# A fused state-space, attention and feed-forward layer on one core: merged head transfers, the weights' peaks two chunks sooner, and four smaller moves of work

## The chip, the cores and the metric

The kernel runs on one core of a Trainium2 chip. The metric is the device time of one execution in microseconds; lower is better.

## The reference

The input `x` holds complex weights for 32 images (32 x 128 x 64), `txt` holds 77 rows of 1024 for each image.

```python
h = tok(log_dt, Lambda, x, 1024)          # (32, 128, 1024): real part of sum_n W[n] * exp(dt*Lambda[n]*pos)
h = concatenate([h, txt], axis=1)         # (32, 205, 1024)
h = h + attn(layernorm(h), wq, wk, wv, wo)   # 32 query heads on 8 key/value heads of 32, causal softmax
h = h + ffn(layernorm(h), W_base, b_base, enc0, enc1, coefs, masks)
# ffn: x @ (W_base + low-rank update through a real Fourier matrix).T + b
```

## The kernel before

The program has three stages, each a block of its own with one instruction stream per engine; the streams meet only through semaphores, and each stage begins when all engines have left the one before.

**Stage 1 (`ssm`)** makes the 128 image rows of each of the 32 images. It goes over 16 chunks of 8 rows (`NCH`, `ch`): GpSimd and VectorE form `u` and `es`, TensorE multiplies, ScalarE copies the result into `ob`, and SP stores it to `hcat` with four transfers a chunk (L180). SP also loads `wq`, `wk` and `wv` ahead for stage 2 (L169). In chunks 4 to 15 VectorE takes one twelfth of the weights' absolute maxima each (`weight_peak`, L370), and after chunk 15 reduces them to `peaks` (L388, L389). SP writes `peaks` to memory (L174), waits, and reads them back broadcast to all partitions (L176) in its turn for chunk 15, ahead of that chunk's stores.

**Stage 2 (`attention`)** is a pipeline over the images in steps `b` = -4 to 32. In step b, where the image exists: attention proper of image b (`att`: `scores` L956 and L959, exponentials L758, causal masks L684 on GpSimd, high parts L765 on ScalarE, low parts `pl` L689 on GpSimd for k = 1, 2 and L911 on VectorE for k = 0, products `weigh` L986, `norm` L808 and L811); the row maxima of image b+1 (`max`: `score_rows` L1000 to L1007, `take_maxes` L854 and L860); the projections of image b+2 (`qkv`: `unit` L1018 to L1026); the turned and split x of image b+3 (`turn`); the layer norm of image b+4 (`ln`); the load of image b+5. A number is kept as two float16 parts, a high one and the rest. Each step has eight slots `g`, one per group of four heads. The steps -4 to -1 fill the pipeline, from step 30 on there are no projections, and in step 31 no maxima either.

Projected heads come out of TensorE with 128 features (four heads of 32) on the partitions, in `qsh`, `qsl`, `ksh` and `ksl`; the score products want one head's 32 features three times below each other (high, high, low). SP's `restack` moves them with transfers inside SBUF, one per head r of four and per part k: twelve transfers for each half of q and of k, so 48 a step (L572). The negated maxima (`mh`, `ml`, unit "m") go in as two more rows (`shift_rows`, L617 and L618). All these, the turning transfers (`turn`, L623 and L624) and, in step -1, the loads for stage 3 (`ahead`, L597: wo, 4 MB, and 14 small ones) stand in one order in SP's stream: q and k of the second half, m 1, in step -1 the loads, turn, k and q of the first half, m 0. ScalarE's first part of the norm's split (`high_part`, L717 and L719, slots 4 to 7) overwrites the x that the latest turn reads, and waits for it.

The reciprocal root of the norm starts on VectorE (`rsqrt_guess`, L1108 to L1110) and ends with three rounds of four small instructions and `nmean` on GpSimd (`scale_rows`, L1117 to L1120, L661). In step -4 VectorE then makes the low parts `ql` of wq (`weights_low`, L794), and after them the low parts `xfl` of x (`low_part`, L837); TensorE's first projection in step -2 waits for their turned form. In step 31 VectorE also has `spare_work` for stage 3.

**Stage 3 (`tail`)** goes over 52 tiles of 128 rows: two projections (L1381 to L1383), residual, norm, store.

## Time and profile before

| | |
|---|---|
| median of 3 runs | 2941.69 us (2940.85 to 2944.85) |
| profiled execution | 2947.19 us, its span 2945.1 us |
| TensorE matmul busy | 2695.8 us, 92% |
| VectorE, ScalarE, GpSimd busy | 66%, 41%, 39% |
| stage 1, stage 2, stage 3 | about 0 to 187, 187 to 1797, 1797 to 2945 us |
| granted TensorE clock, mean | 0.969 |

The span runs from the first to the last instruction. A granted clock of 1.00 is TensorE's full speed of 2.4 GHz, 0.50 is 1.2 GHz. Matmuls overlap and their ends are modelled, so a busy share near 100% is not the array at its peak. In a row of the timeline the columns are the start, the time, the engine, the line with its operation, what is written and read, the count, and in brackets how long the engine sat idle before it and what ended that. SPq and ACTq rows are the issue of a transfer, not its course.

### The profile page before, as it was taken

What the parts mean: (1) busy time and instruction counts of PE and PEld (TensorE: products, weight loads), DVE (VectorE), ACT (ScalarE), POOL (GpSimd) and SP (SyncE); (2) the same over time, 40 slices, a digit from 0 to 9 for tenths busy, and PEclk for the clock granted to TensorE, in tenths of its full rate; (3) what the DMA queues carried; (4) which work ended last, traced back from release to release, by engine and by line L of the source; (5) the groups of instructions that cost most, each with busy time, mean ns of one, the idle gap of its engine ahead of it and who ended that gap; (6) DMA issues with size and microseconds to landing.
All of it is one profiled execution on the core that took longest, in us unless ns stands there. A gap on an engine that the chain in (4) does not pass through costs nothing. (4 is left out here: it accounts for less than half of the span.)

```text
span 2945.1 us, 70977 instructions
## 1 busy us (share of the span) xinstructions
PE 2695.8 (92%) x27456; PEld 1949.7 (66%) x27456; DVE 1940.4 (66%) x5569; ACT 1201.6 (41%) x2506; POOL 1144.2 (39%) x1811
## 2 busy tenths in 40 slices
PE   1948699999999999999999986999999999999999
PEld 1837589989898998989899972444444444444444
DVE  8964488887888888788888774744444444444443
ACT  4342466676766767666666663101010100101010
POOL 2751266565656656566565563101111010101110
PEclk9978899999999999999999995899999999999999
DMA  7754534434343443435344325354554555454543
GB/s 240 190 123 112 87 88 96 98 77 98 82 102 85 93 98 77 99 82 103 81 95 87 66 55 178 79 139 115 136 123 128 131 119 134 119 140 115 136 122 81
DMA packets 564334, 324.72 MB, mean 110 GB/s; under 512 B 501016, under 2 KB 519704, under 8 KB 563520
## 3 DMA queue, kind: packets, MB, share of 16 engines
q1 hardware_dynamic: 541488, 256.35, 39.2%
q10 hardware_dynamic: 22512, 63.84, 6.9%
q8 instruction: 219, 3.59, 0.5%
q14 instruction: 115, 0.94, 0.1%
HBM read 116.49 MB, written 80.61 MB: 67 GB/s over the span
## 5 line engine op out<-in xcount | busy, mean ns | idle before, releaser
L1018 PE MATMUL psJ<-xth,qh 128*128 128x205 f16 x2048 | 520.3, 254 | 52.4 <-DMA xtl<-xfl 46.9
L689 POOL TENSOR_TENSOR pl<-arena,ph 128x410 f16<-128x410 f32 (+1 forms) x512 | 499.5, 995 | 94.7 <-ACT ph L765 94.7
L1020 PE MATMUL psJ<-xth,ql 128*128 128x205 f16 x2048 | 519.0, 253 | 0.0
L1019 PE MATMUL psJ<-xtl,qh 128*128 128x205 f16 x2048 | 518.6, 253 | 0.0
L684 POOL TENSOR_SCALAR_AFFINE_SELECT arena<-arena 128x256 f32<-128x256 f32 (+1 forms) x768 | 331.6, 438 | 475.5 <-ACT arena L758 454.5
L1243 POOL TENSOR_TENSOR arena<-stage,arena 128x1024 f32<-128x1024 f32 x52 | 122.2, 2349 | 938.1 <-DVE stage L1286 938.1
L1257 ACT CAST xh<-arena 128x1024 f16<-128x1024 f32 x52 | 54.3, 1045 | 998.3 <-DVE arena L1295 998.3
L758 ACT ACTIVATE arena<-psT,escale 128x410 f32<-128x410 f32 (+1 forms) x768 | 401.1, 567 | 119.0 <-PE psT L959 59.7
L765 ACT CAST ph<-arena 128x410 f16<-128x410 f32 (+1 forms) x768 | 334.8, 500 | 15.8 <-POOL arena L684 15.5
L1286 DVE SCALAR_TENSOR_TENSOR stage<-ps5O,osc,h_in 128x512 f32<-128x512 f32 x104 | 78.0, 751 | 390.6 <-PE ps5O L1383 390.6
L860 DVE TENSOR_REDUCE mx<-psS 77x2 f32<-77x410 f32 x512 | 295.4, 577 | 39.8 <-PE psS L1007 32.3
L1381 PE MATMUL ps5F<-wfh,xth 128*128 128x512 f16 x832 | 315.4, 379 | 3.1 <-DMA xtl<-xl 2.0
L1382 PE MATMUL ps5O<-wol,ath 128*128 128x512 f16 x832 | 316.3, 380 | 0.0
L1381 PE MATMUL ps5O<-woh,ath 128*128 128x512 f16 x832 | 316.3, 380 | 0.0
L1383 PE MATMUL ps5O<-woh,atl 128*128 128x512 f16 x832 | 316.2, 380 | 0.0
L854 DVE CUSTOM_DVE_ANT_0 seen<-psS,mask 128x128 bf16<-128x128 f32 x1024 | 235.3, 286 | 121.5 <-PE psS L1000 121.5
L1382 PE MATMUL ps5F<-wfl,xth 128*128 128x512 f16 x832 | 315.3, 379 | 0.0
L1383 PE MATMUL ps5F<-wfh,xtl 128*128 128x512 f16 x832 | 315.3, 379 | 0.0
L986 PE MATMUL psO<-vh,ph 128*128 128x33 f16 (+1 forms) x3072 | 261.2, 178 | 5.1 <-issue 4.7
L986 PE MATMUL psO<-vl,ph 128*128 128x33 f16 (+1 forms) x3072 | 260.4, 178 | 0.0
L986 PE MATMUL psO<-vh,pl 128*128 128x33 f16 (+1 forms) x3072 | 260.4, 178 | 0.0
L986 PEld LDWEIGHTS psO<-vh,ph 128*128 128x128 f16 (+1 forms) x3072 | 245.2, 97 | 7.3 <-issue 6.3
(234 smaller groups left out, 6143.7 us busy)
## 6 DMA issues: line engine op xcount, KB each, us to landing
a_in<-acat SPq DMA_DIRECT2D x52, 512.0 KB, 3.8
h_in<-hcat SPq DMA_DIRECT2D x52, 512.0 KB, 4.6
qst<-qsh SPq DMA_DIRECT2D x512, 51.2 KB, 2.1
out<-stage SPq DMA_DIRECT2D x51, 512.0 KB, 3.1
hcat<-ob SPq DMA_DIRECT2D x64, 256.0 KB, 4.5
xin<-hcat ACTq DMA_DIRECT2D x32, 512.0 KB
acat<-arena ACTq DMA_DIRECT2D x64, 256.0 KB
qst<-qsl SPq DMA_DIRECT2D x256, 51.2 KB, 2.5
```

The costliest lines, as they stand in the source:

```text
L684: pool.affine_select(out=v, in_=v, compare_op=ALU.is_ge, fill=0.0, base=0, pattern=[[0, v.shape[1]], [1, w]], channel_multiplier=-1).then_ ...
L689: pool.tensor_tensor(view(pl, g % 2, k), view(p32, g % 2, k), view(ph, g % 2, k), ALU.subtract).then_inc(lo_pool, 1)
L758: act.activation(view(p32, g % 2, k), ps_view(psT[(g + k) % 2], k), ACT.Exp, scale=(escale[:, 0:1] if k < 2 else escale[0:TXT, 0:1])).then ...
L765: act.copy(view(ph, g % 2, k), view(p32, g % 2, k)).then_inc(hi_done, 1)
L860: dve.tensor_reduce(dst, v, AX.X, ALU.max).then_inc(s_read, 1)
L986: m = pe.matmul(o[:, t, r, :], p, v[0:T[j], j, g, :], start=n == 0, stop=n == len(list_) - 1)
L1018: pe.matmul(ps[:, 0:S], wh[:, k, c], xth[:, par, k, 0:S], start=k == 0, stop=False)
L1019: pe.matmul(ps[:, 0:S], wh[:, k, c], xtl[:, par, k, 0:S], start=False, stop=False)
L1020: m = pe.matmul(ps[:, 0:S], wl[:, k, c], xth[:, par, k, 0:S], start=False, stop=k == KC - 1)
L1381: pe.matmul(ps[h][:], th[:, k, :], wh[:, k, c], start=k == 0, stop=False)
L1382: pe.matmul(ps[h][:], th[:, k, :], wl[:, k, c], start=False, stop=False)
L1383: m = pe.matmul(ps[h][:], tl[:, k, :], wh[:, k, c], start=False, stop=k == KC - 1)
```

## The change

- **Merged head transfers.** The columns of `wq` and `wk` are laid out, ahead of the launch, so that a chunk's partitions hold feature and head as d*4 + r. `restack` then moves a whole part with one transfer: 3 for a half of q or k, 12 a step, each of the bytes of four before. `qst` is laid out as [half, r, c] and `mx` likewise, so the operands of `scores` for two heads become two runs of 205 columns.
- **Peaks.** The twelve reductions stand in chunks 2 to 13, the two final ones at the end of chunk 13; SP writes the peaks ahead of chunk 14's stores and reads them back ahead of chunk 15's.
- **First root.** In step -4 the three rounds and `nmean` are VectorE's, right behind the guess; GpSimd does none in that step.
- **Loads for stage 3.** They stand in step 1 instead of step -1, between m 1 and the turn as before.
- **Last steps.** In steps 30 and 31 (`LATE` on) the low part for k = 1 is VectorE's (`lo_late`), GpSimd keeps k = 2.

```diff
             for ch in range(NCH):
-                if ch == NCH - 1:
+                if ch == NCH - 2:
                     sp.wait_ge(peaks_ok, 1)
                     sp.dma_start(acat[0, 0:2 * P].rearrange("(p t) -> p t", t=2), peaks[:]).then_inc(peaks_out, 16)
+                if ch == NCH - 1:
                     sp.wait_ge(peaks_out, 16)
...
                 dve.tensor_tensor(u[:, ch % 2], u[:, ch % 2], u2[:, ch % 2], ALU.add).then_inc(u_ok, 1)
-                if ch >= NCH - 12:
-                    weight_peak(ch - (NCH - 12))
-            dve.wait_ge(piece_ok, 12)
-            dve.tensor_reduce(peaks[:, 0:1], pieces[:, 0:8], AX.X, ALU.max)
-            dve.tensor_reduce(peaks[:, 1:2], pieces[:, 8:12], AX.X, ALU.max).then_inc(peaks_ok, 1)
+                if NCH - 14 <= ch < NCH - 2:
+                    weight_peak(ch - (NCH - 14))
+                if ch == NCH - 3:
+                    dve.wait_ge(piece_ok, 12)
+                    dve.tensor_reduce(peaks[:, 0:1], pieces[:, 0:8], AX.X, ALU.max)
+                    dve.tensor_reduce(peaks[:, 1:2], pieces[:, 8:12], AX.X, ALU.max).then_inc(peaks_ok, 1)
...
         mh, ml = sb("mh", [NH // 2, 2, S], F16), sb("ml", [NH // 2, 2, S], F16)
-        qst = [sb(f"qst{i}", [STACK + 2, NH, S], F16) for i in range(2)]
+        qst = [sb(f"qst{i}", [STACK + 2, 2, REP, NKV // 2, S], F16) for i in range(2)]
         kst = [sb(f"kst{i}", [STACK + 2, NKV, S], F16) for i in range(2)]
...
         pl = sb("pl", [P, 2, 3, 2 * S], F16)
-        mx = sb("mx", [P, 2, NH])
+        mx = sb("mx", [P, 2, 2, REP, NKV // 2])
         seen = sb("seen", [P, REP, P], BF16)
...
         cleared, lo_pool, mask_ok, late_ok = sem("cleared"), sem("lo_pool"), sem("mask_ok"), sem("late_ok")
+        lo_late = sem("lo_late")
         pool_c, dve_c, dve_ln, const_ok = sem("pool_c3"), sem("dve_c3"), sem("dve_ln"), sem("const_ok")
...
+        LATE = B - 2
+        def by_pool(n):
+            return 2 * n - max(0, n - 8 * LATE)
...
             if kind == "q":
-                wait(eng, q_in[n // 4], 16 * 12 * (b + 2))
+                wait(eng, q_in[n // 4], 16 * 3 * (b + 2))
             if kind == "k":
-                wait(eng, k_in[n], 16 * 12 * (b + 2))
+                wait(eng, k_in[n], 16 * 3 * (b + 2))
             if kind == "v":
...
                 for k, src in enumerate(parts_):
-                    rows = dst[k * HD:(k + 1) * HD].rearrange("d (c r) i -> d c r i", r=4)
-                    for r in range(4):
-                        sp.dma_start(rows[:, cs, r, :], src[r * HD:(r + 1) * HD, cs, :]).then_inc(arrived, 16)
+                    sp.dma_start(dst[k * HD:(k + 1) * HD], src[:, cs, :]).then_inc(arrived, 16)
...
                     wait(sp, pj_lo, before(b - 1, nxt) + at(units(prev), "k", 1) + 1)
-                    restack(K_PARTS, kst[nxt], slice(1, 2), k_in[1])
+                    restack(K_PARTS, kst[nxt][:, 4:8], slice(1, 2), k_in[1])
                     wait(sp, pj_lo, before(b - 1, nxt) + at(units(prev), "q", NKV - 1) + 1)
-                    restack(Q_PARTS, qst[nxt], HALVES[1], q_in[1])
+                    restack(Q_PARTS, qst[nxt][:, 1], HALVES[1], q_in[1])
                 if has["att"]:
...
                     shift_rows(1, par)
-                if b == -1:
-                    sp.wait_ge(w_lo, 2 * KC)
+                if b == 1:
...
                     wait(sp, st_filled, 24 * b + 12)
-                    restack(K_PARTS, kst[par], slice(0, 1), k_in[0])
+                    restack(K_PARTS, kst[par][:, 0:4], slice(0, 1), k_in[0])
                     wait(sp, pj_lo, base + at(rows, "q", 3) + 1)
-                    restack(Q_PARTS, qst[par], HALVES[0], q_in[0])
+                    restack(Q_PARTS, qst[par][:, 0], HALVES[0], q_in[0])
                 if has["max"]:
...
             def shift_rows(half, to):
-                heads = slice(half * (NH // 2), (half + 1) * (NH // 2))
-                sp.dma_start(qst[to][STACK:STACK + 1, heads, :], mh[:, half, :]).then_inc(m_in[half], 16)
-                sp.dma_start(qst[to][STACK + 1:STACK + 2, heads, :], ml[:, half, :]).then_inc(m_in[half], 16)
+                sp.dma_start(qst[to][STACK:STACK + 1, half], mh[:, half, :]).then_inc(m_in[half], 16)
+                sp.dma_start(qst[to][STACK + 1:STACK + 2, half], ml[:, half, :]).then_inc(m_in[half], 16)
...
                 if not has["att"]:
-                    if has["ln"]:
+                    if has["ln"] and b > -4:
                         scale_rows(b)
...
                                            channel_multiplier=-1).then_inc(masked, 1)
-                    for k in (1, 2):
+                    for k in (1, 2) if b < LATE else (2,):
                         pool.wait_ge(hi_done, 24 * b + 3 * g + k + 1)
...
-                            if k:
-                                wait(act, lo_pool, 16 * b + 2 * (g - 2) + k)
+                            last = 8 * b + g - 2
+                            if k == 1 and last >= 8 * LATE:
+                                act.wait_ge(lo_late, last + 1 - 8 * LATE)
+                            elif k:
+                                wait(act, lo_pool, by_pool(last + 1) - 2 + k)
                             else:
...
                     rsqrt_guess(chain, dve, rs, mv[:, :, 1])
+                    if b == -4:
+                        rsqrt_rounds(link, dve, rs)
+                        dve.tensor_scalar(nmean[:], mv[:, :, 0], -1.0, None, ALU.mult).then_inc(ln_done, 1)
...
                             m = dve.tensor_tensor_reduce(seen[:, r, :], src[:, r * P:(r + 1) * P], mask[:, 0, :], 1.0, LEAST,
-                                                         ALU.add, ALU.max, mx[:, 0, 4 * j + r:4 * j + r + 1])
+                                                         ALU.add, ALU.max, mx[:, 0, j // 4, r, j % 4:j % 4 + 1])
                         m.then_inc(s_read, 1)
...
                         v = src[0:TXT, 0:2 * S].rearrange("p (h i) -> p h i", i=S)
-                        dst = mx[0:TXT, 1, 4 * j + 2 * k - 2:4 * j + 2 * k]
+                        dst = mx[0:TXT, 1, j // 4, 2 * k - 2:2 * k, j % 4]
                         dve.tensor_reduce(dst, v, AX.X, ALU.max).then_inc(s_read, 1)
...
                                           ALU.subtract).then_inc(lo_done, 1)
+                        if b >= LATE:
+                            dve.wait_ge(hi_done, 24 * b + 3 * g + 2)
+                            dve.tensor_tensor(view(pl, g % 2, 1), view(p32, g % 2, 1), view(ph, g % 2, 1),
+                                              ALU.subtract).then_inc(lo_late, 1)
                     for j in groups[1:]:
...
                 if k < 2:
-                    m = pe.matmul(ps[:, 0:2 * S], K[:, g, 0:P], Q[:, 4 * g + 2 * k:4 * g + 2 * k + 2, :],
+                    m = pe.matmul(ps[:, 0:2 * S], K[:, g, 0:P], Q[:, g // 4, 2 * k:2 * k + 2, g % 4, :],
                                   start=True, stop=True)
                 else:
-                    m = pe.matmul(ps[0:TXT, 0:REP * TXT], K[:, g, P:S], Q[:, 4 * g:4 * g + 4, P:S],
+                    m = pe.matmul(ps[0:TXT, 0:REP * TXT], K[:, g, P:S], Q[:, g // 4, :, g % 4, P:S],
                                   start=True, stop=True)
...
                 pe.wait_ge(lo_done, 8 * b + g + 1)
-                pe.wait_ge(lo_pool, 16 * b + 2 * g + 2)
+                pe.wait_ge(lo_pool, by_pool(8 * b + g + 1))
+                if b >= LATE:
+                    pe.wait_ge(lo_late, 8 * (b - LATE) + g + 1)
...
-                pe.wait_ge(q_in[j // 4], 16 * 12 * (b + 1))
-                pe.wait_ge(k_in[j // 4], 16 * 12 * (b + 1))
+                pe.wait_ge(q_in[j // 4], 16 * 3 * (b + 1))
+                pe.wait_ge(k_in[j // 4], 16 * 3 * (b + 1))
                 K, Q = kst[par], qst[par]
...
                     for r in range(REP):
-                        m = pe.matmul(ps[:, r * P:(r + 1) * P], Q[0:STACK, 4 * j + r, 0:P], K[0:STACK, j, 0:P],
+                        m = pe.matmul(ps[:, r * P:(r + 1) * P], Q[0:STACK, j // 4, r, j % 4, 0:P], K[0:STACK, j, 0:P],
                                       start=True, stop=True)
...
                     for r in range(2):
-                        m = pe.matmul(v[:, r, :], Q[0:STACK, 4 * j + 2 * (k - 1) + r, P:S], K[0:STACK, j, :],
+                        m = pe.matmul(v[:, r, :], Q[0:STACK, j // 4, 2 * (k - 1) + r, j % 4, P:S], K[0:STACK, j, :],
                                       start=False, stop=r == 1, skip_group_check=True)
...
-                    heads = slice(n * (NH // 2), (n + 1) * (NH // 2))
                     pe.wait_ge(s_read, 24 * (b + 1) + 12 * (1 - n))
-                    pe.transpose(ps[0:NH // 2, 0:P], mx[:, 0, heads], ident[:])
-                    m = pe.transpose(ps[0:NH // 2, P:S], mx[0:TXT, 1, heads], ident[0:TXT, 0:TXT])
+                    pe.transpose(ps[0:NH // 2, 0:P], mx[:, 0, n].rearrange("p r c -> p (r c)"), ident[:])
+                    m = pe.transpose(ps[0:NH // 2, P:S], mx[0:TXT, 1, n].rearrange("p r c -> p (r c)"), ident[0:TXT, 0:TXT])
                 if last:
...
             a = a.T
+        if name in ("L0_attn_wq", "L0_attn_wk"):
+            a = a.reshape(D, -1, 4, HD).transpose(0, 1, 3, 2).reshape(D, -1)
         a = np.ascontiguousarray(a)
```

## Rows read from the trace of the kernel before

**Rows 1.** Busy time in a stretch of the steady steps.

```profile
core 0: us, PE busy (x) PEld busy (x) DVE busy (x) ACT busy (x) POOL busy (x), PEclk, DMA share, GB/s
700.00:1000.00 300.00, 287.44 (x4374) 267.98 (x4372) 246.33 (x841) 197.97 (x447) 182.52 (x334) 1.00 0.41 88
```

**Rows 2.** TensorE's waits, whole span: total, times, longest.

```profile
PE psJ L1018 <- DMA xtl<-xfl: 46.9, 1, 46.9
PE psS L1004 <- DVE mx L854: 43.4, 64, 1.1
...
PE psT L956 <- DMA qst<-ml: 16.8, 2, 12.1
PE psS L1004 <- DVE mx L860: 14.0, 1, 14.0
```

**Rows 3.** Timeline, steps -1 and 0: TensorE, VectorE and SP's queue.

```profile
266.13 0.61 PE L1000 MATMUL psS<-kst,qst 96*128 96x128 f16 x4 [5.89 <-DMA qst<-qsl]
...
280.74 0.59 SPq L597 DMA_DIRECT2D stage<-in_L_attn_wo  x1
...
282.88 11.87 SPq L597 DMA_DIRECT2D mk<-in_L_ffn_mask  x1
...
294.89 0.35 DVE L866 SCALAR_TENSOR_TENSOR ml<-psJ,mh 16x205 f16<-16x205 f32 x1
...
305.80 1.28 SPq L623 DMA_TRANSPOSE xth<-xfh  x1
...
327.74 0.59 SPq L618 DMA_DIRECT2D qst<-ml  x1
```

**Rows 4.** Timeline of ScalarE: the first high part in steps -1, 0, 1.

```profile
310.62 0.72 ACT L717 ACTIVATE xin<-xin,nmean 128x512 f32<-128x512 f32 x1 [17.17 <-DMA xtl<-xfl]
...
362.19 0.70 ACT L717 ACTIVATE xin<-xin,nmean 128x512 f32<-128x512 f32 x1
...
408.68 0.71 ACT L717 ACTIVATE xin<-xin,nmean 128x512 f32<-128x512 f32 x1
```

**Rows 5.** Timeline, step 1: ml of slot 0, and its issue.

```profile
386.26 0.35 DVE L866 SCALAR_TENSOR_TENSOR ml<-psJ,mh 16x205 f16<-16x205 f32 x1
...
390.55 0.60 SPq L617 DMA_DIRECT2D qst<-mh  x1
```

**Rows 6.** Timeline, step -4: VectorE and GpSimd.

```profile
198.29 0.19 DVE L1110 TENSOR_SCALAR rs<-rs 128x2 int32<-128x2 int32 x1
198.52 9.65 DVE L794 SCALAR_TENSOR_TENSOR ql<-stage,qsc,qh 128x1024 f16<-128x1024 f32 x8
198.59 1.26 POOL L1117 TENSOR_TENSOR rs<-rs 128x2 f32<-128x2 f32 x1
...
209.41 0.25 POOL L661 TENSOR_SCALAR nmean<-mv 128x2 f32<-128x2 f32 x1
...
215.36 0.75 DVE L837 SCALAR_TENSOR_TENSOR xfl<-xin,rs,xfh 77x512 f16<-77x512 f32 x1 [0.62 <-ACT xfh L719]
```

**Rows 7.** Timeline, end of stage 1: ScalarE and SP's queue.

```profile
178.04 0.59 ACT L246 COPY ob<-ps 128x512 f32<-128x512 f32 x1 [1.14 <-PE ps L401]
179.63 0.34 SPq L176 DMA_DIRECT2D arena<-acat  x1
180.02 3.19 SPq L180 DMA_DIRECT2D hcat<-ob  x4
```

**Rows 8.** Busy time after a wait, in a slot of step 30, in step 31.

```profile
266.00:275.00 9.00, 8.87 (x66) 7.96 (x67) 3.17 (x13) 0.69 (x2) 0.00 (x0) 0.66 0.11 25
...
1739.20:1742.40 3.20, 2.51 (x57) 1.95 (x54) 3.06 (x14) 2.76 (x7) 2.87 (x6) 1.00 0.33 79
1765.50:1789.50 24.00, 15.74 (x272) 9.18 (x271) 20.69 (x35) 19.69 (x43) 21.84 (x35) 0.50 0.11 37
```

**Rows 9.** All instructions of L911: nanoseconds min/median/max, first and last start.

```profile
L911 DVE TENSOR_TENSOR pl<-arena,ph x256: 562/586/1690, 334.7 to 1789.4; 128x410 f16<-128x410 f32 x128
```

**Rows 10.** Transfers: count, KB each, us from issue to landing.

```profile
qst<-qsh SPq DMA_DIRECT2D x512, 51.2 KB, 2.1
...
hcat<-ob SPq DMA_DIRECT2D x64, 256.0 KB, 4.5
```

## The prediction

> **What bounds the kernel.** I read the windows first. In the middle of attention TensorE is busy 287.4 of 300 us at the full clock [rows 1]; each step there takes 46.5 us, the distance between the same ScalarE instruction of two steps [rows 4]. Nothing can be gained there except what TensorE waits for, so the second view is the list of its waits [rows 2]. Of these only one belongs to the steady steps, the 43.4 us for L854 (64 times, two a step, about 0.7 us each), and the change doesn't shorten what L854 does. Its waits on a transfer are few and long: they stand at the start (46.9 us for the first turned x, 12.1 for ml, and 5.9 for qsl [rows 3]), and one of 4.7 us (16.8 less 12.1) for ml again, which is at the end. The third view, the timeline with SP's queue, says why: a restack is 12 issues of some 0.65 us, and SP does nothing else meanwhile; in step -1 the loads that are needed only 1.4 ms later are put between two restacks and hold the queue from 280.7 to 305.8 us [rows 3]. ScalarE then waits 17.2 us for the turned x behind them [rows 4], and TensorE 14.0 us through L860 [rows 2]. The steady steps hide the SP queue, the fill doesn't.
>
> **The change, part by part** (minus is a gain).
>
> 1. *Peaks sooner.* SP writes the peaks after chunk 14's rows, waits, reads them at 179.63 and starts chunk 15's four stores at 180.02, while ScalarE's last copy was done at 178.04 + 0.59 = 178.63 [rows 7]. The round trip now lies one chunk ahead, so the stores start at 178.7: -1.3. The reductions move two chunks ahead, where VectorE has as much room; the first needs wq, whose load I take as landed; if it were not, the cost is that lateness less VectorE's idle time. I put 0 on it.
>
> 2. *First root on VectorE.* GpSimd's thirteen small steps run from 198.59 to 209.66; the first took 1.26 us beside VectorE [rows 6]. VectorE's own step on two columns takes 0.19 us, 0.23 from start to start, so thirteen take about 2.9 us and ScalarE can begin 8 us sooner. But VectorE does them ahead of its eight ql parts (9.65 us), which stand before its first xfl. Before, the last xfl ended at 216.1 [rows 6]; now the root ends at 198.5 + 2.9 = 201.4, ql at 211.1, and four xfl (0.75 us each, about 0.66 from start to start) at 213.7. The same 2.4 us pass on to kl, to the second image's norm and to TensorE's second start. Gain -2.4, not 8; bounds 0 and -8.
>
> 3. *Merged restacks.* One restack becomes 3 issues; at 0.65 us an issue that is 2 us instead of 8. At the start, TensorE waits 5.9 us for qsl [rows 3]; this restack and the one ahead of it shrink by 6 us each, so the wait is gone: -5.9. The wait for ml (12.1) starts after step -1's work. Step -1 began at 266.1; ml was ready at 295.2, 29.1 us later, yet went out at 327.7 behind turn and restacks [rows 3]. It lands about 2 us after, so the wait began near 317.6, and TensorE's own work in this step is 317.6 - 266.1 - 14.0 = 37.5 us. With the queue free, mh and ml are issued (1.2) and landed (2) at 29.1 + 3.2 = 32.3 us, ahead of 37.5: -12.1. In the steady steps the gain is 0, because no wait on a transfer stands there to be shortened. What lies behind 0: SP ended its steady restack at 390.55 without anybody waiting [rows 5].
>
> 4. *Small loads leave step -1.* The 25 us of SP go, so ScalarE's wait goes and TensorE's with it: -14.0 [rows 2, 4].
>
> 5. *Clock.* After the 5.9 us wait TensorE ran nine microseconds at a mean clock of 0.66 [rows 8]: 9 x 0.34 = 3.1 us lost. The lower level is 0.50, 1.2 GHz. This restart goes (-3.0); the two others end in short or stalled work, and I take -1.5 each: -6.0.
>
> 6. *Small loads come into step 1.* This is the cost. SP takes them up when mh and ml of slot 0 are ready, 386.6 us on the old time axis, and not at 390.55, since its restack is shorter [rows 5]. Two issues 1.2, then the loads. Before, from the first of these loads to ScalarE's release were 310.62 - 280.74 = 29.9 us [rows 3, 4]. Release: 386.6 + 1.2 + 29.9 = 417.7. ScalarE wants that turned x at 408.68 [rows 4]: 9.0 us late. In step -1 17.2 us of ScalarE's wait became 14.0 of TensorE's; here the next exponentials stand behind the waiting instruction, and I take 8.0, between 6 (the same slack of 3.2) and 9. The wait lets the clock fall: a restart as in part 5, 2.5. Sum +10.5. The restack and mh, ml behind the loads would be 9 us late too, but TensorE's next step is then 8 us late itself. The bound below is 0 (the loads drain quicker), above 17 + 3 (the stall of step -1 again).
>
> 7. *Two last steps.* TensorE's 4.7 us wait for ml [rows 2], which SP issues behind a restack, goes, with 1.5 of clock: -6.2. Against it, in step 30 VectorE is busy 3.06 of 3.20 us of a slot, GpSimd 2.87 [rows 8]. Taking a low part (1.0 us) off GpSimd while VectorE gains one of 0.586 us [rows 9], 0.54 taken, since starts follow a little closer than durations, makes VectorE the bound: 8 x 0.54 = +4.3. In step 31 VectorE was busy 20.7 of 24.0 us; with seven or eight more it needs 24.7, while GpSimd falls well below its 21.8 [rows 8]. I take 0, between -3 (GpSimd alone had set the pace) and +2. Part: -1.9; bounds -9 and +0.
>
> The two-piece operand of L956 (two runs of 205 instead of one of 410), the strided writes into mx, and the permuted weights, which are laid out ahead of the launch, I cost at 0: no row shows such a run, the nearest are the steady waits, which leave TensorE no stall there. Above it 2 us.
>
> One rule speaks against part 3. The Trainium skill, "DMA: Bandwidth & Descriptors", section Issuing engines are not separate DMA queues, says that the time a sequencer needs to initiate a DMA is usually small relative to the DMA. Here the queue's rows say otherwise: issues of 0.65 us one after another, landing 2.1 us after each [rows 10]. By the rule parts 3 and 5 would shrink; it is a rival below.
>
> **Sum.** -1.3 - 2.4 - 5.9 - 12.1 - 14.0 - 6.0 + 10.5 - 1.9 = -33.1. The profiled execution took 2947.2 (span 2945.1), which gives 2914.1; the runs' median is 2941.7, 0.2% lower, so 2941.7 - 33.1 = 2908.6.
>
> **Rivals.**
>
> A. *The loads are free in step 1.* The queue in a steady step carries less once restacks are merged. Then part 6 is 0: 2898. Against it: the 4 MB alone blocked SP for 11.9 us in one issue [rows 3].
>
> B. *The next wait takes over in the fill.* VectorE and ScalarE have long serial stretches there, and part 3's 12.1 or part 4's 14.0 could be half eaten: +9, or the loads cost the full 17 + 3 in step 1 (+10): 2917.
>
> C. *Bytes, not issues.* A merged transfer lands as late as its four pieces did; parts 3 and 5 give nothing (22 us back): 2930. This is the rule cited above. For it: DMA engines are busy 41% in the steady window [rows 1]. Against: 256 KB of hcat land in 4.5 us, 51 KB in 2.1 [rows 10].
>
> D. *VectorE and GpSimd hold each other up in the last steps.* One L911 took 1.69 us instead of 0.586 [rows 9]. If all 16 new ones did, +17: 2925. The Trainium skill, "SBUF — State Buffer", section SBUF: two separate sides, calls the port pair that both share an exclusive lock; the 1.69 us agrees with that, the median of 0.586 says that it is rare.
>
> E. *The other side: slower.* A merged transfer moves at the rate of one small one, 4 x 2.1 = 8.4 us, and six a step, one after another, need 50.4 us against a step of 46.5 [rows 4, 10]: +3.9 in 30 steps, less the gain of the fill: about 3025. It decides from 7.9 us a transfer, (46.5 + 1.1) / 6. Against it the 4.5 us for 256 KB.
>
> F. *It doesn't do what it says:* something else in the fill (the first weights, the first norm) ends each wait, all within 5 us of before: 2938.
>
> **How the numbers follow.** Forecast 0.50 (own range 2901 to 2915), A 0.16, B 0.14, C 0.05, D 0.08, E 0.04, F 0.03. The range of 8 in 10 holds the forecast, A and B with the bounds of parts 6 and 7: 2894 to 2921. A measurement here tells 0.2%, 5.9 us, from no change. Faster: all but E and F, 0.93; within: F, 0.03; slower: E, 0.04.
>
> **What would show it.** SP's restacks as 3 issues, about 2 us; the loads in step 1 with a new wait of ScalarE of about 9 us at its high part and of TensorE of about 8, at half clock after it; no wait of TensorE on ml or qsl; L860's 14.0 gone; ScalarE's first xfh some 10 us sooner but TensorE's first projection only 3 to 4; a slot of step 30 at 3.7 us with VectorE without idle time. The prediction is wrong if the steady steps change from 46.5 us (E, or a gain that I exclude), if the new wait in step 1 is under 4 or over 14, or if step -1 keeps a wait of more than 5 us.

## The result and the profile after

The changed kernel takes 2913.9 us in the median of 4 runs (2910.36 to 2916.59); the kernel before took 2943.27 beside it (2940.85 to 2945.48). The ratio is 0.99 with an interval of 0.9883 to 0.9917, a gain of 29.4 us. The profiled spans are 2945.1 and 2911.4 us, 33.7 apart; the forecast was 33.1 off the profiled time.

TensorE's waits over the whole span, the view of [rows 2], now for the changed kernel:

```profile
PE psJ L1040 <- DMA xtl<-xfl: 46.6, 1, 46.6
PE psS L1026 <- DVE mx L870: 45.7, 65, 1.1
PE psT L979 <- ACT arena L770: 25.6, 42, 11.8
PE psO L1008 <- DVE pl L931: 7.4, 6, 2.0
```

L1026, L870 and L979 are the L1004, L854 and L959 of before. The waits for ml and qsl and the 14.0 us behind L860 are gone. One is new: 11.8 us for ScalarE's exponentials (L770). SP's queue and ScalarE in step 1 of the changed kernel show where it comes from, in the columns of [rows 3]:

```profile
344.68 0.58 SPq L626 DMA_DIRECT2D qst<-mh  x1
...
345.94 1.20 SPq L607 DMA_DIRECT2D stage<-in_L_attn_wo  x1
...
348.91 11.77 SPq L607 DMA_DIRECT2D mk<-in_L_ffn_mask  x1
360.73 5.77 SPq L607 DMA_DIRECT2D cf<-in_L_ffn_coefs  x1
...
373.47 1.28 SPq L632 DMA_TRANSPOSE xth<-xfh  x1
...
378.92 0.64 SPq L583 DMA_DIRECT2D kst<-ksh  x1
379.60 0.60 SPq L583 DMA_DIRECT2D kst<-ksl  x1
380.25 0.60 SPq L583 DMA_DIRECT2D kst<-ksh  x1
```
```profile
378.30 0.72 ACT L726 ACTIVATE xin<-xin,nmean 128x512 f32<-128x512 f32 x1 [11.47 <-DMA xtl<-xfl]
```

The reader sees three things. A restack of k is three issues of 0.6 us. The loads hold the queue for 27.5 us (345.94 to 373.47), much as they did in step -1 (25.1, [rows 3]). And ScalarE, which waits for nothing else, stands 11.5 us for the turned x behind them.

To place gains I use one mark that every kernel has, ScalarE's mh, which is written once for each half of an image's maxima: the second half early in the image's own step, the first half late in the step before. Here are its rows in the changed kernel, for the second half of images 0, 1 and 2 (steps 0, 1 and 2), the first half of image 29 (late in step 28) and the second half of image 31 (step 31):

```profile
296.00 0.33 ACT L783 ACTIVATE mh<-psJ 16x205 f16<-16x205 f32 x1
...
342.47 0.33 ACT L783 ACTIVATE mh<-psJ 16x205 f16<-16x205 f32 x1
...
402.27 0.33 ACT L783 ACTIVATE mh<-psJ 16x205 f16<-16x205 f32 x1
...
1638.87 0.33 ACT L783 ACTIVATE mh<-psJ 16x205 f16<-16x205 f32 x1 [0.45 <-PE psJ L1056]
...
1728.49 0.33 ACT L783 ACTIVATE mh<-psJ 16x205 f16<-16x205 f32 x1
```

The table takes the distances between such rows, for all kernels that ran ("projection" is the start of TensorE's first projection of x; "step 2 to 29" ends at the mark late in step 28, some 26.5 steps on; "rest" is the span less the mark of step 31, which stands where that step begins, so step 31 itself lies in the rest). The distance from step 0 to step 1 is 46.5 us in all.

| kernel | projection | step 0 | step 1 to 2 | step 2 to 29 | step 29 to 31 | rest |
|---|---|---|---|---|---|---|
| before | 224.91 | 337.93 | 46.68 | 1241.76 | 92.58 | 1179.7 |
| changed | 223.51 | 296.00 | 59.80 | 1236.60 | 89.62 | 1182.9 |
| loads_back | 228.50 | 311.74 | 46.96 | 1237.07 | 90.86 | 1178.1 |
| loads_end0 | 225.64 | 296.44 | 47.70 | 1237.04 | 90.52 | 1178.3 |
| low_on_gpsimd | 227.16 | 298.70 | 59.64 | 1238.05 | 86.28 | 1176.8 |
| end0_low | 226.18 | 298.01 | 47.20 | 1236.31 | 86.29 | 1180.1 |
| four_pieces | 224.15 | 310.84 | 67.71 | 1238.11 | 93.66 | 1178.4 |
| merge_only | 221.65 | 309.62 | 46.59 | 1239.44 | 86.29 | 1176.0 |
| before_loads1 | 225.11 | 313.57 | 67.63 | 1241.46 | 94.10 | 1176.3 |
| memset_wait | 221.53 | 294.40 | 59.71 | 1235.89 | 90.85 | 1178.2 |
| best | 220.01 | 291.93 | 46.59 | 1236.22 | 86.34 | 1179.5 |
| best_root_gpsimd | 223.54 | 297.70 | 46.48 | 1236.73 | 86.32 | 1179.8 |

From before to changed: -41.9 at step 0, +13.1 from step 1 to 2, -5.2 over the steady steps, -3.0 at the end, +3.2 in the rest: with a step of rounding, the 33.7 us of the spans.

### The profile page after: what moved, and what is told of

The parts are those of the page before. It is cut to its first block and busy times, and to the rows that moved or that the text cites. A ratio compares the mean times of both kernels' runs of the same rounds, so it can differ in the third digit from the quotient of the medians.

```text
span 2911.4 us, 69838 instructions
## 1 busy us (share of the span) xinstructions
PE 2689.6 (92%) x27456; PEld 1945.8 (67%) x27456; DVE 1955.2 (67%) x5598; ACT 1202.3 (41%) x2506; POOL 1125.5 (39%) x1782
## 3 DMA queue, kind: packets, MB, share of 16 engines
q1 hardware_dynamic: 449328, 256.28, 42.1%
## 5 line engine op out<-in xcount | busy, mean ns | idle before, releaser
L1040 PE MATMUL psJ<-xth,qh 128*128 128x205 f16 x2048 | 518.1, 253 | 49.6 <-DMA xtl<-xfl 46.6
L698 POOL TENSOR_TENSOR pl<-arena,ph 128x410 f16<-128x410 f32 (+1 forms) x496 | 489.8, 1006 | 100.5 <-ACT ph L777 100.5
L770 ACT ACTIVATE arena<-psT,escale 128x410 f32<-128x410 f32 (+1 forms) x768 | 402.0, 566 | 113.1 <-PE psT L979 60.0
L777 ACT CAST ph<-arena 128x410 f16<-128x410 f32 (+1 forms) x768 | 334.8, 500 | 12.4 <-POOL arena L693 12.1
L876 DVE TENSOR_REDUCE mx<-psS 77x2 f32<-77x410 f32 x512 | 296.5, 579 | 44.2 <-PE psS L1029 37.5
L870 DVE CUSTOM_DVE_ANT_0 seen<-psS,mask 128x128 bf16<-128x128 f32 x1024 | 235.4, 286 | 98.2 <-PE psS L1022 98.2
L1008 PEld LDWEIGHTS psO<-vh,ph 128*128 128x128 f16 (+1 forms) x3072 | 245.6, 97 | 10.5 <-DVE pl L927 8.4
## 6 DMA issues: line engine op xcount, KB each, us to landing
qst<-qsh SPq DMA_DIRECT2D x128, 205.0 KB, 4.7
qst<-qsl SPq DMA_DIRECT2D x64, 205.0 KB, 5.6
```

What stands on the lines that cost most here:

```text
L698: pool.tensor_tensor(view(pl, g % 2, k), view(p32, g % 2, k), view(ph, g % 2, k), ALU.subtract).then_inc(lo_pool, 1)
L770: act.activation(view(p32, g % 2, k), ps_view(psT[(g + k) % 2], k), ACT.Exp, scale=(escale[:, 0:1] if k < 2 else escale[0:TXT, 0:1])).then ...
L777: act.copy(view(ph, g % 2, k), view(p32, g % 2, k)).then_inc(hi_done, 1)
L876: dve.tensor_reduce(dst, v, AX.X, ALU.max).then_inc(s_read, 1)
L1008: m = pe.matmul(o[:, t, r, :], p, v[0:T[j], j, g, :], start=n == 0, stop=n == len(list_) - 1)
L1040: pe.matmul(ps[:, 0:S], wh[:, k, c], xth[:, par, k, 0:S], start=k == 0, stop=False)
```

## The experiments

The kernel before was run again beside them: it took 2943.36 us (9 runs) beside the first four, 2941.01 (21) beside four_pieces, merge_only, before_loads1 and memset_wait, and 2943.39 (9) beside best and best_root_gpsimd. Ratios are against these. Diffs are against the changed kernel unless said otherwise.

### loads_back: the small loads in step -1 again

```diff
-                if b == 1:
+                if b == -1:
+                    sp.wait_ge(w_lo, 2 * KC)
                     for dst, src, arrived in ahead:
```

> The changed kernel with the loads for stage 3 back in step -1; merged restacks stay. Theory (SP's queue sets the waits): the loads now start near 257 us instead of 281, ScalarE's turned x is released 29.9 us later, near 287, about 7 us after it is due, and mh, ml of the first image land near 297; step 0 begins at 296 to 298 instead of 287.5, and the 11.8 us wait in step 1 is gone. Against before -33 us (2910), 3 to 4 us faster than the changed kernel. Rival (my part 4: the loads in step -1 cost their 14.0 whatever the restacks are): step 0 begins at 301 or later, against before -28 or less.

Measured: 2913.48 us (2909.81 to 2914.54), ratio 0.9889 (0.9876 to 0.9903). The step 0 mark comes 15.7 us later than in the changed kernel, and 12.8 of the 13.1 us in step 1 are saved. 5.0 of the 15.7 us stand ahead of the first projection, which this edit doesn't touch. A move that I counted at -14 + 10.5 is worth nothing here. Neither theory nor rival came out whole: step 0 began at 303.7, as the rival had it (298.7 without those 5.0 us), the gain over the kernel before is 29.9 us, and the kernel is 0.4 us faster than the changed one and not 3 to 4. TensorE's waits in this kernel:

```profile
PE psT L979 <- ACT arena L770: 12.0, 42, 0.9
PE psS L1026 <- DVE mx L876: 7.6, 1, 7.6
```

Even with the loads back in step -1, the 14.0 us behind L860 have become 7.6 (L876 is that line), for SP, with less to issue ahead of them, reached the loads at 260.4 instead of 280.7:

```profile
260.44 0.61 SPq L607 DMA_DIRECT2D stage<-in_L_attn_wo  x1
...
262.69 10.67 SPq L607 DMA_DIRECT2D mk<-in_L_ffn_mask  x1
...
288.55 1.27 SPq L632 DMA_TRANSPOSE xth<-xfh  x1
```

### loads_end0: the same loads at the end of SP's turn in step 0

```diff
-                if b == 1:
-                    for dst, src, arrived in ahead:
-                        sp.dma_start(dst, src).then_inc(arrived, 16)
...
                 if has["max"]:
                     wait(sp, pj_lo, base + at(rows, "m", 0) + 1)
                     shift_rows(0, nxt)
+                if b == 0:
+                    for dst, src, arrived in ahead:
+                        sp.dma_start(dst, src).then_inc(arrived, 16)
```

> The changed kernel with the loads for stage 3 at the end of step 0's turn in SP's queue, behind mh and ml of slot 4, instead of step 1's between mh, ml and the turn. Theory (the loads block what stands right behind them, and behind that place there are some 20 us of room): no wait of TensorE over 3 us in steps 0 to 2, step 0 still begins at 287.5; 13 us faster than the changed kernel, -42 against before (2901). Rival (the bytes of the loads hold up the transfers behind them wherever they stand): ScalarE still waits over 5 us for a turned x, gain over the changed kernel under 6.

Measured: 2901.42 us (2898.64 to 2903.98), ratio 0.9851 (0.9837 to 0.9865), 12.5 us under the changed kernel. SP's queue in this kernel:

```profile
324.10 0.59 SPq L622 DMA_DIRECT2D stage<-in_L_attn_wo  x1
...
326.20 10.31 SPq L622 DMA_DIRECT2D mk<-in_L_ffn_mask  x1
...
347.81 0.68 SPq L622 DMA_DIRECT2D mk<-in_L_ffn_mask  x1
348.59 0.62 SPq L583 DMA_DIRECT2D kst<-ksh  x1
...
353.84 1.28 SPq L631 DMA_TRANSPOSE xth<-xfh  x1
```

The loads begin 22 us earlier than in the changed kernel, in time that the queue would have idled or spent on restacks with slack (there it did nothing from 323.6 to 331.4), so the turn goes out at 353.8 and not at 373.5. The distance from step 1 to 2 is 47.7 us against 46.7 before: the loads now cost 1 us (47.2, 46.6 and 46.5 in the three other kernels that have them here).

### low_on_gpsimd and end0_low: the low parts stay on GpSimd

```diff
-        LATE = B - 2
+        LATE = B
```

end0_low has this edit and that of loads_end0.

> The changed kernel with all low parts for k = 1 and 2 on GpSimd again, in steps 30 and 31 too. Theory (VectorE is the bound in both steps): a slot of step 30 takes 3.2 us instead of 3.6 to 4.1, TensorE's clock stays up in it, step 31 takes 28.4 instead of 29.7; 4 to 6 us faster than the changed kernel, -34 against before. Rival (GpSimd was the bound in these steps, moving work off it paid): 1 to 4 us slower than the changed kernel.

> Both of the two edits before: loads at the end of step 0, low parts on GpSimd. They lie 1.3 ms apart, so the theory has them add up: 17 to 19 us faster than the changed kernel, -47 against before (2896). If either rival holds, its part is missing: -34 or -42.

Measured: 2907.3 us (2905.27 to 2911.28), ratio 0.9872 (0.9858 to 0.9887), and 2894.86 (2893.68 to 2899.69), ratio 0.9831 (0.9817 to 0.9845). Each is 6.6 us under its counterpart with VectorE's low parts. In the table the last steps take 86.3 us in the five kernels with merged restacks and the low parts on GpSimd, and 89.6 to 90.9 in the four with them on VectorE. Windows over step 30 of the changed kernel and over the same step of low_on_gpsimd, in the columns of [rows 1]:

```profile
1698.60:1728.50 29.90, 23.81 (x421) 17.87 (x417) 27.20 (x107) 23.36 (x53) 22.27 (x32) 0.80 0.23 47
```
```profile
1702.00:1728.50 26.50, 20.69 (x428) 16.09 (x427) 23.49 (x99) 23.11 (x52) 23.79 (x41) 1.00 0.27 59
```

With the low parts on VectorE it is busy 27.2 of 29.9 us; with them on GpSimd no engine is busy over 23.8 of 26.5. TensorE's granted clock averages 0.80 in the first and 1.00 in the second. The low parts themselves were not held up, as all instructions of their line show (nanoseconds min/median/max):

```profile
L931 DVE TENSOR_TENSOR pl<-arena,ph x16: 567/576/855, 1699.4 to 1754.7; 128x410 f16<-128x410 f32 x16
```

### four_pieces: the merged layout, but twelve issues again

```diff
-                    sp.dma_start(dst[k * HD:(k + 1) * HD], src[:, cs, :]).then_inc(arrived, 16)
+                    for i in range(4):
+                        if cs.stop - cs.start == 4:
+                            c = cs.start + i
+                            sp.dma_start(dst[k * HD:(k + 1) * HD, :, i, :], src[:, c, :]).then_inc(arrived, 16)
+                        else:
+                            sp.dma_start(dst[k * HD + 8 * i:k * HD + 8 * i + 8], src[32 * i:32 * i + 32, cs, :]).then_inc(arrived, 16)
```

> The changed kernel with each merged restack issued in four pieces again: the same bytes, layout and packets as the merged ones, but twelve issues a half-step where the changed kernel has three. Theory (what the merging bought is SyncE's issue time, about 0.65 us for each of the issues taken away): the restacks take about 8 us a half-step again, TensorE waits some 4 us for the q rows at the start of step -1 and some 8 us for ml, and the 5 us that the steady steps gained are gone (from the first mh of step 2's second half to that of step 29's first half 1286 us, not 1281); so 8 to 10 us under the kernel before, 2934. Rival (the gain comes from the landing of the merged layout, not from the issues): the time stays at the changed kernel's, 2914.

Measured: 2945.33 us (2937.38 to 2947.69), ratio 1.0013 (1.0004 to 1.0022): all of the gain is gone, and more than I expected. The bytes and the layout are those of the changed kernel, so the rival falls. The packets are not, against what the expectation says: SP's queue moved 535344 here and 449328 in the changed kernel. That the time goes by issues and not by packets or bytes is seen in the issues themselves, which take 0.6 us each whether they carry 51.2 or 205.0 KB. TensorE's waits in this kernel:

```profile
PE psT L984 <- ACT arena L775: 26.0, 41, 13.7
...
PE psT L981 <- DMA qst<-ml: 12.9, 3, 5.0
...
PE psS L1027 <- DMA qst<-qsl: 6.3, 1, 6.3
```

Against the changed kernel the table has +14.8 us at step 0, +7.9 from step 1 to 2 (here SP reaches the loads later, and they cost 21.0 us instead of 13.1), +1.5 over the steady steps and +4.0 at the end. The 1286 and 1281 us of the expectation end one image later, at the mark late in step 29: that distance is 1286.0 us before, 1280.8 in the changed kernel and 1282.3 here, so of the steady gain of 5 us, which I had expected to go, 1.5 went. On the whole I had expected 11 us less. 7.9 us that I hadn't counted are the loads' cost in step 1, which I took as independent of the issues; the rest is not placed, for its profiled execution was the quickest of its runs, 8 us under the median, and its span understates it.

### merge_only: nothing but the merging

```diff
-                if ch == NCH - 2:
+                if ch == NCH - 1:
...
-                if NCH - 14 <= ch < NCH - 2:
-                    weight_peak(ch - (NCH - 14))
-                if ch == NCH - 3:
+                if NCH - 12 <= ch:
+                    weight_peak(ch - (NCH - 12))
+                if ch == NCH - 1:
...
-                if b == 1:
+                if b == -1:
+                    sp.wait_ge(w_lo, 2 * KC)
...
-                    if has["ln"] and b > -4:
+                    if has["ln"]:
...
-                    if b == -4:
-                        rsqrt_rounds(link, dve, rs)
-                        dve.tensor_scalar(nmean[:], mv[:, :, 0], -1.0, None, ALU.mult).then_inc(ln_done, 1)
```

(and LATE = B as above)

> The changed kernel with all else put back: small loads in step -1, low parts on GpSimd up to the end, the first root on GpSimd, the weights' peaks in chunks 4 to 15. Only the merged restacks are left. Theory (once the restacks are merged, the loads' place, the root and the low parts give nothing or cost): -33 us against the kernel before, about 2910, no slower than the whole change. Rival (the parts add up as I predicted: without the loads' move, the root and the low parts the merging alone is worth less): above 2920.

Measured: 2905.05 us (2903.98 to 2906.5), ratio 0.9877 (0.9863 to 0.989). Merging alone gains 36.0 us, against 29.4 for the whole change. The step 0 mark is 28.3 us earlier than before, the last steps are 6.3 us shorter, the steady steps 2.3; behind the first projection no wait of over 6 us is left in the fill.

### before_loads1: the loads' move alone

Against the kernel before:

```diff
-                if b == -1:
-                    sp.wait_ge(w_lo, 2 * KC)
+                if b == 1:
```

> The kernel before with one edit: the small loads issued in step 1 in place of step -1, the restacks unmerged. Theory (the loads' step costs the step that takes them, wherever it is, and with the long restacks it costs more in step 1 because SyncE's turn is longer there): 25 us less at the end of step 0, 13 to 27 us more in step 1: 2943, within 4 us of the kernel before. Rival (my prediction's parts 4 to 6, which were summed as if independent of the merging): -14 -1.5 +10.5, 5 us or more under it, 2938 or less.

Measured: 2941.67 us (2935.04 to 2945.89), ratio 0.9999 (0.999 to 1.0008). 24.4 us are won at step 0 and 21.0 lost from step 1 to 2. TensorE's waits:

```profile
PE psT L958 <- ACT arena L757: 30.8, 47, 14.4
...
PE psT L955 <- DMA qst<-ml: 13.8, 3, 4.9
PE psS L999 <- DMA qst<-qsl: 6.3, 1, 6.3
```

The 12.1 us for ml are gone here with the restacks unmerged (the longest wait is 4.9): the loads and the restacks had made that wait together, and either edit takes most of it.

### memset_wait: GpSimd's memset behind the root

In the changed kernel one of VectorE's small steps in the first root took some 25 times as long as the others. VectorE, then GpSimd:

```profile
195.33 0.16 DVE L1139 TENSOR_TENSOR rs<-rs 128x2 f32<-128x2 f32 x1
195.53 4.18 DVE L1140 TENSOR_SCALAR rs<-rs 128x2 f32<-128x2 f32 x1
199.74 0.16 DVE L1141 TENSOR_TENSOR rs<-rs 128x2 f32<-128x2 f32 x1
...
210.37 2.73 DVE L853 SCALAR_TENSOR_TENSOR xfl<-xin,rs,xfh 128x512 f16<-128x512 f32 x4
```
```profile
195.43 2.17 POOL L679 MEMSET ph<- 128x2460 f16 x1
197.54 2.14 POOL L680 MEMSET pl<- 128x2460 f16 x1
```

The edit, ahead of the memset of ph:

```diff
+                        pool.wait_ge(ln_done, 1)
```

> The changed kernel with one wait more: GpSimd's memset of ph and pl in step -4 waits for the end of the first root's rounds on VectorE. Theory (the VectorE instruction of 4.18 us among rounds of 0.16 us is held up by GpSimd's memsets): that instruction takes 0.2 us, the first TensorE projection begins 4 us sooner (about 219.5 us), and so does step 0; 4 us under the changed kernel, 2910. Rival (the next wait takes over: the q weights or the turned x are late anyway, or the memset itself comes late): under 1 us.

Measured: 2908.45 us (2907.46 to 2911.4), ratio 0.989 (0.9876 to 0.9903). The same instruction takes 0.17 us, as its fellows do:

```profile
196.11 0.16 DVE L1140 TENSOR_TENSOR rs<-rs 128x2 f32<-128x2 f32 x1
196.30 0.17 DVE L1141 TENSOR_SCALAR rs<-rs 128x2 f32<-128x2 f32 x1
```

The projection starts 2.0 us sooner than in the changed kernel, and 4.7 sooner than the mean of the five kernels with the collision in one piece (226.2, the changed kernel among them). (The sixth, four_pieces, started it at 224.15.) By the times alone it can't be told from the changed kernel, since the two intervals overlap; the trace shows the mechanism.

### best and best_root_gpsimd: the parts that paid, together

best is end0_low with memset_wait's edit. best_root_gpsimd is end0_low with the first root back on GpSimd:

```diff
-                    if has["ln"] and b > -4:
+                    if has["ln"]:
...
-                    if b == -4:
-                        rsqrt_rounds(link, dve, rs)
-                        dve.tensor_scalar(nmean[:], mv[:, :, 0], -1.0, None, ALU.mult).then_inc(ln_done, 1)
```

> The merged restacks, the small loads at the end of SyncE's turn in step 0, the low parts on GpSimd to the end, the first root on VectorE and GpSimd's first memset behind its rounds. Theory (the memset's collision with the root is worth its 4 us here too): 4 us under the same kernel without the wait, 2891. Rival (the turned x comes late for another reason, and the first projection begins no more than 2 us sooner): 2893 to 2895.

> The kernel best with the first root computed on GpSimd, as in the kernel before, and no extra wait. Theory (from the last of the root's start values on VectorE to the last low part of x, 17.6 us passed with the root on GpSimd, 18.8 with it on VectorE beside GpSimd's memsets, 15.0 with the memset held back): 2.6 us later than best at the first projection, so 2 to 3 us over best in the span. Rival (nothing of it reaches the end, the run to run spread of stage 1 is larger): within 1 us of best.

Measured: 2888.45 us (2888.07 to 2890.11), ratio 0.9817 (0.9803 to 0.983), 54.9 us under the kernel before; and 2893.78 (2889.3 to 2895.62), ratio 0.9829 (0.9816 to 0.9843). The runs of the two overlap a little at 2889 to 2890, and their profiled spans are 2887.1 and 2893.5. best is 6.4 us under end0_low, where I had expected 4. The two lie 5.3 us apart, where I had expected 2 to 3: from the end of the guess to the last xfl it is 14.8 against 17.6 us, 2.8 as expected, and the rest is not explained. best_root_gpsimd and end0_low are 1.1 us apart with overlapping intervals: with the collision, no gain from the root on VectorE is shown. TensorE's waits in best:

```profile
PE psJ L1040 <- DMA xtl<-xfl: 43.2, 1, 43.2
...
PE psT L979 <- ACT arena L770: 17.2, 46, 1.8
```

## Why the prediction was right, and where it was not

The forecast of 2908.6 us lies 5.3 under the median, in its own range, and the range of 8 in 10 holds the result. The mechanism ahead of step 0 was right in the main: the waits named are gone, and where parts 1 to 5 summed to -41.7, the mark in step 0 moved -41.9. That the two agree to 0.2 us is luck. Ahead of the first projection, where parts 1 and 2 had -3.7, it moved -1.4; from there to step 0, where parts 3 to 5 had -38.0, -40.5. The -1.4 is itself a lucky draw: in the six kernels with the root on VectorE and the memsets beside it the projection starts at 223.51 (the changed kernel) to 228.50, 225.9 in the mean, and before it started at 224.91. The agreement of the whole hides several terms that were off.

1. *Peaks sooner* (-1.3). This came as worked. SP starts chunk 15's stores at 177.54, 0.03 us after ScalarE's last copy ends at 177.51, where it was 1.39 us after before (178.63 to 180.02, [rows 7]): -1.4 for -1.3. With the peaks early that distance is 0.02 to 0.03 us in all nine kernels, with them late 1.2 to 1.4 in the three. That the copy itself ended 1.1 us sooner doesn't go with the edit: its end lies between 177.3 and 179.4 in the twelve kernels, earliest in merge_only, which has the peaks late.

```profile
176.93 0.58 ACT L247 COPY ob<-ps 128x512 f32<-128x512 f32 x1 [1.14 <-PE ps L403]
177.54 3.02 SPq L181 DMA_DIRECT2D hcat<-ob  x4
```

2. *First root on VectorE* (-2.4). The order of work was right: root, then ql, then xfl. From the end of the guess to the end of the last xfl, it took 17.6 us before (198.48 to 216.11, [rows 6]), and 18.8 in the changed kernel (194.31 to 213.10), because one instruction stood 4.2 us beside GpSimd's memsets. With the memset held back (memset_wait) it took 14.8, from 195.09 to 209.87: -2.8 for the -2.4 as worked. The term that failed is the duration of the thirteen steps, 2.9 us expected and 6.5 measured: in the changed kernel part 2 gave a loss of 1.2 us there and not a gain. I had thought of two engines holding each other up for the last steps only, as rival D; it struck here.

3. and 4. *Merged restacks* (-5.9 -12.1) and *small loads leave step -1* (-14.0). The sum was right, the shares were not. From projection to the step 0 mark it is 113.0 us before, 88.0 with merging alone, 88.5 with the move alone, 72.5 with both: each alone is worth 25, together 40.5. So 9 us, most of them the wait for ml, could be had by either, and I had given them to the merging. That matters for the next step.

5. *Clock* (-6.0). No restart is left in step -1: the granted clock was 0.66 over nine microseconds [rows 8], now it is 1.00 in a window of the same length. How much of the step 0 gain is clock can be read from TensorE's busy time between the first projection and the mark of step 0, for the same 723 matmuls: 76.35 us before and 68.31 now, 8.0 less where I had 6.0. The other 32.5 of the 40.5 us are idle time. (The ends of matmuls are modelled, so the split is rough.) The kernel before, then the changed one, whose last two rows are for part 5 and part 6:

```profile
224.91:337.93 113.02, 76.35 (x723) 71.64 (x724) 43.18 (x149) 28.76 (x59) 11.76 (x45) 0.81 0.44 101
```
```profile
223.51:296.00 72.49, 68.31 (x723) 65.49 (x724) 42.59 (x147) 28.79 (x59) 10.99 (x41) 0.97 0.55 92
...
256.00:265.00 9.00, 8.78 (x92) 8.45 (x92) 6.37 (x21) 1.31 (x4) 0.00 (x0) 1.00 1.05 153
...
378.50:390.00 11.50, 9.68 (x137) 8.79 (x138) 6.10 (x18) 9.75 (x20) 5.94 (x10) 0.71 0.68 123
```

6. *Small loads come into step 1* (+10.5). It cost 13.1. ScalarE was 11.5 us late and not 9.0, nearly all of it came through to TensorE (11.8, not 8.0), and the clock after it, 0.71 over 11.5 us in the last row above, took 3.3 and not 2.5. The two make 15.1, 2.0 more than the step grew by, so a part of it was made up within the step. With the unmerged restacks it would have been 21.0. Parts 4 and 6 together gave -3.5 in my sum; measured with merged restacks the pair is worth nothing (loads_back), nor without them (before_loads1). A stall was moved and not removed; at the end of step 0 it is removed.

7. *Two last steps* (-1.9, made of -6.2 and +4.3). Merging alone shortens them by 6.3 us (merge_only): the first term stands. VectorE's low parts cost 3.3 to 4.6 in the table. In step 30 itself, where I had said slots of 3.7 us (they were 3.6), VectorE's first low part goes from 1698.87 to 1727.84 in eight slots, 28.97 us, in low_on_gpsimd 25.62 (1702.86 to 1728.48): +3.4 for +4.3. I had 0.54 us a slot and no clock. The two slots before the clock fell took 3.6 us each against 3.2, so 0.4 a slot; the next three, at 0.50, took 3.8 to 4.1. Windows on both sides of the fall in the changed kernel:

```profile
1702.80:1706.20 3.40, 2.21 (x46) 1.69 (x44) 3.27 (x15) 2.85 (x6) 2.72 (x5) 1.00 0.36 113
1706.20:1709.60 3.40, 3.00 (x37) 2.18 (x34) 3.01 (x14) 2.33 (x5) 2.82 (x4) 0.51 0.03 5
```

For step 31 I took 0; its first five slots took 19.42 us and in low_on_gpsimd 17.57: +1.9. The part's sign was right, but I didn't draw the conclusion: it was two edits, of which one was a loss.

*The steady steps* (0) were not untouched: 5.2 us less over some 26.5 steps, 0.2 a step. I had excluded any gain there and named a change from 46.5 us as a sign of being wrong, so this term of 0 failed, though by little. A possible cause is ScalarE's own transfer issues. In the kernel before, ScalarE's queue and ScalarE:

```profile
1160.95 0.33 ACTq L705 DMA_DIRECT2D acat<-arena  x1
1161.32 2.01 ACTq L706 DMA_DIRECT2D acat<-arena  x1
1163.43 1.53 ACT L758 ACTIVATE arena<-psT,escale 128x410 f32<-128x410 f32 x3 [1.76 <-issue]
```

An issue that takes 0.4 us as a rule took 2.01 and held the exponentials back. Summed from 285 to 1785 us, ScalarE's issues take 80.6 and 79.4 us in the two kernels with 12 issues in the old layout, where the steady steps take 1241.8 and 1241.5; 75.6 and 75.5 in merge_only and four_pieces (1239.4, 1238.1); and 72.4 and 72.1 in the changed kernel and in memset_wait (1236.6, 1235.9). In the six others they take 72.1 to 74.7 (1236.2 to 1238.1). The two go together, but no run changed this alone. four_pieces speaks against SP's issues as the whole cause: it has all twelve of them again and keeps 3.7 of the 5.2 us. The cause is left open.

*The rest* cost 3.2 us, of which step 31 is 1.9. It differs by 6.9 us (1176.0 to 1182.9) among kernels whose stage 3 is the same, so I read no more from it.

Of the rivals, A (free loads) is refuted by the 13.1 us. The row that I held against it was misread: the issue of 11.87 us in [rows 3] is one of `mk`, a small load; the 4 MB of wo took 0.59 to issue. Whether they are what held `mk` back, no run tested.

C (bytes, not issues) is refuted by four_pieces; parts 3 and 5, which it gives back, are 24.0 us together and not 22. The rule of the Trainium skill, "DMA: Bandwidth & Descriptors", section Issuing engines are not separate DMA queues, that the time of initiating a DMA is usually small beside it, doesn't fit here: an issue takes 0.65 us and lands after 2.1, and with the bytes unchanged, nine more issues a restack cost 31 us in all (2945.33 less 2913.9; 33 by the ratios). One half of C did come, that a merged transfer lands about as late as the last of its four pieces. The page of the changed kernel has its count, bytes and time to landing:

```profile
qst<-qsh SPq DMA_DIRECT2D x128, 205.0 KB, 4.7
```

One merged transfer lands 4.7 us after its issue. A piece of a quarter of its bytes took 2.1 [rows 10], so the last of four, issued some 1.95 us after the first, landed at 4.1 by this estimate. What is won lies between the transfers: for a whole restack of q it is 10.2 us from the first issue to the last landing before and 6.9 now, and SP's queue is held for 8.6 before and 1.9 now (medians of 64). E's 8.4 us didn't come, nor the 7.9 from which it would have decided. Of the 10 us of B's larger price in step 1, 2.6 came (part 6). D struck in step -4. In the last steps none of the 16 new low parts took over 0.86 us (L931 above); one of the old ones took 1.78, as one did before (1.69, [rows 9]).

## What to carry to other kernels

Work that holds a queue is not removed by moving it: look for the stretch in which that queue idles and nobody needs what stands behind, and try the move alone, for two edits that cut one wait share its gain. Undo a mixed change part by part even when its sum came out as forecast: here one of five parts gave more than the whole. When small steps are moved to VectorE, look at what GpSimd does in those microseconds.

## What the hardware showed beyond expectation

- A VectorE TENSOR_SCALAR on two columns took 4.18 us instead of 0.17 while GpSimd ran two memsets of 2.1 us each, and ended as the second did (199.71 and 199.68). Five more kernels had it (3.96 to 4.39 us, once in two pieces of 2.10 and 1.49), three of them on the same step and two on an int32 TENSOR_SCALAR of the guess; in the changed kernel the TENSOR_TENSOR steps beside it kept their 0.16 us. With the memsets later it was gone. The Trainium skill, "SBUF — State Buffer", section SBUF: two separate sides, has the port pair of the two engines as an exclusive lock; these rows agree with it.
- One load of `mk` held SP's queue for 9.8 to 12.2 us in all twelve kernels, whether it stood in step -1, 0 or 1.
- TensorE's granted clock fell to 0.50 from 1706.2 to 1716.5 us in step 30 of the changed kernel without a long wait ahead of it: the longest from the step's start to the fall was 1.15 us, ending at 1705.15, and TensorE was busy 2.21 of the last 3.40 us. In low_on_gpsimd, with slots of 3.2 us, it stayed at 1.00. The busy shares of the two windows over the step don't compare the work, since matmuls at the lower clock last longer (one of L1026 0.23 us at 1.00 and 0.32 to 0.34 at 0.50; 421 matmuls in 29.90 us and 428 in 26.50).
